# A routed feed-forward layer: constants built earlier, rows added per round of gathers, attention of four batches interleaved on three engines

## The reference

```python
x = x + 0.5 * _L0_ffn_ref(_layernorm(x), ...)   # first FFN
x = x + _L0_attn_ref(_layernorm(x), ...)        # full attention, 8 heads over 2048 tokens
x = x + 0.5 * _L0_ffn_ref(_layernorm(x), ...)   # second FFN

def _L0_ffn_ref(x, ...):                         # x: 8 batches, 2048 tokens, 256 wide
    scores = x @ w_router
    _, idx = jax.lax.top_k(scores, CAP)          # 128 tokens of each batch
    x_sel = jnp.take_along_axis(x, idx[:, :, None], axis=1)
    h = rmsnorm(x_sel, g1)
    q, k, v = ...                                # h @ W_qkv.T, 16 heads of 16
    att = softmax(where(mask, -inf, q @ k.T / 4))
    x_attn = (att @ v) @ W_out.T
    h2 = rmsnorm(x_sel + x_attn, g2)
    x_ff = silu(h2 @ W1.T) * (h2 @ W2.T) @ W3.T
    return x.at[..., idx].set(x_sel + x_attn + x_ff)
```

## Time and profile before

| | us |
|---|---|
| median of 3 runs | 4640.27 (4639.2 to 4641.36) |
| the profiled execution | 4629.35 |
| its span | 4627.6 |
| first `routed_ffn` in the span | 202.2 to 466.0 |
| second `routed_ffn` in the span | 4349.9 to 4627.6 |

### The profile page before, as it was taken

The page is one execution under the profiler, slowest core; times in us unless marked ns, Lnnn a source line. Parts: engine busy times, 40 slices in busy tenths (PEclk is TensorE's granted clock), DMA queues, the critical chain, the costliest instruction groups (busy, mean ns, idle before and its releaser), DMA issues. The chain is left out here.

```text
span 4627.6 us, 72033 instructions
## 1 busy us (share of the span) xinstructions
PE 3742.8 (81%) x21202; PEld 1462.9 (32%) x21202; DVE 3268.7 (71%) x4504; ACT 3216.1 (69%) x6587; POOL 2553.0 (55%) x966
## 2 busy tenths in 40 slices
PE   0176576599999999999999999999999999930276
PEld 0143354133333333333333333333333333310143
DVE  8644465777777877777777777778777777648544
ACT  5143365488888888878888887888888888834043
POOL 0011000377777777776777777677767777754111
PEclk9988788699999999999999999999999999965588
DMA  8200599677878878777887888788787877678100
GB/s 273 74 5 5 208 344 336 138 146 167 175 160 170 177 158 178 168 168 157 169 169 162 177 169 169 155 169 176 156 178 167 169 165 167 130 214 305 43 5 5
DMA packets 326047, 743.31 MB, mean 161 GB/s; under 512 B 26060, under 2 KB 209888, under 8 KB 270112
## 3 DMA queue, kind: packets, MB, share of 16 engines
q0 software_dynamic: 57216, 407.92, 44.3%
q1 hardware_dynamic: 234880, 297.04, 21.6%
q10 hardware_dynamic: 33568, 33.69, 2.1%
HBM read 198.90 MB, written 136.48 MB: 72 GB/s over the span
## 5 line engine op out<-in xcount | busy, mean ns | idle before, releaser
L1653 ACT ACTIVATE at_probs<-at_ps_s 128x512 f32<-128x512 f32 x4096 | 2255.7, 613 | 346.1 <-PE at_ps_s L1774 261.1
L1538 DVE TENSOR_REDUCE at_part_max<-at_ps_max 128x3 f32<-128x1536 f32 x1024 | 1801.0, 1759 | 472.3 <-PE at_ps_max L1687 464.2
L1516 POOL TENSOR_TENSOR at_pool_sum<-at_pool_sum,at_probs 128x2048 f32<-128x2048 f32 x384 | 1771.9, 4614 | 624.4 <-DMA at_probs<-at_probs 623.4
L1774 PE MATMUL at_ps_s<-at_qs,at_ks 97*128 97x512 f32 (+1 forms) x4096 | 1532.9, 452 | 41.2 <-ACT at_probs L1653 21.4
L1721 PE MATMUL at_ps_acc<-at_probs,at_v 128*32 128x512 f32 x8192 | 1097.5, 608 | 0.9 <-ACT at_probs L1653 0.9
L1774 PEld LDWEIGHTS at_ps_s<-at_qs,at_ks 97*128 97x128 f32 (+1 forms) x4096 | 629.8, 188 | 1151.2 <-ACT at_probs L1653 823.5
L1540 DVE TENSOR_REDUCE at_part_max<-at_max_copy 128x1 f32<-128x512 f32 x1024 | 691.6, 675 | 0.0
L1602 ACT COPY at_max_copy<-at_ps_max 128x512 f32<-128x512 f32 x1024 | 610.0, 596 | 88.1 <-PE at_ps_max L1687 87.6
L1687 PE MATMUL at_ps_max<-at_ks,at_qs 32*128 32x512 f32 x4096 | 525.9, 501 | 68.5 <-DMA at_ks<-qk_parts 34.8
L1493 POOL DMA_DIRECT2D at_probs<-at_probs x384 | 346.1, 901 | 220.6 <-PE at_ps_acc L1721 213.6
L1687 PEld LDWEIGHTS at_ps_max<-at_ks,at_qs 32*128 32x128 f32 x4096 | 198.1, 183 | 425.3 <-issue 363.9
(11 more groups left out here) (195 smaller groups left out, 2723.4 us busy)
## 6 DMA issues: line engine op xcount, KB each, us to landing
at_probs<-at_probs POOLq DMA_DIRECT2D x384, 1024.0 KB, 8.3
qk_parts<-pr_hi SPq DMA_DIRECT2D x32, 1024.0 KB, 6.4
qk_parts<-pr_lo SPq DMA_DIRECT2D x32, 1024.0 KB, 6.1
at_qs<-qk_parts SPq DMA_DIRECT2D x320, 64.0 KB, 6.0
at_ks<-qk_parts SPq DMA_DIRECT2D x80, 256.0 KB
s_x<-in_x SPq DMA_DIRECT2D x16, 1024.0 KB, 8.6
after_ffn<-s_y ACTq DMA_DIRECT2D x16, 1024.0 KB, 6.5
pr_x<-after_ffn SPq DMA_DIRECT2D x8, 2048.0 KB
```

The costliest lines, as they stand in the source:

```text
L1516: nc.gpsimd.tensor_tensor(acc, a, probs[:, c % RING], ALU.add).then_inc(pool_added, 1)
L1538: nc.vector.reduce_max(part_max[:, 0:HG - 1, t, c], ps_max[:, 0:HG - 1], AX.X).then_inc(three_max_done, 1)
L1653: nc.scalar.activation(probs[:, c % RING, h], ps_s[:, BANK[j]], ACT.Exp, scale=SCALE).then_inc(exp_done, 1)
L1774: nc.tensor.matmul(ps_s[:, BANK[j]], ks[rows, g, h, c * P:(c + 1) * P], qs[rows, un % NQB, h, :], start=True, stop=True).then_inc(scores, 1)
```

## The change

Three edits. The constants are tiles of `FfnWeights` and are built on GpSimd at the start of `pick_tokens`. In `routed_ffn` GpSimd gathers the four batches of round 0, adds them where there is something to add, and then does the same for round 1. In the attention part the order of the queues is changed: ScalarE takes the exponentials of slots 0, 1, 2, the copies of slot 0, the exponentials of slot 3, and the copies of slots 1, 2, 3; TensorE does the scores of slots 0, 1, 2, the probabilities of slot 0, the scores of slot 3, and the probabilities of slots 1, 2, 3; VectorE does `outputs(0)` and `outputs(1)` after `normalize(2)` and `normalize(3)`. VectorE also no longer waits for the weights at the start of `routed_ffn`.

```diff
+    def build(self, engine):
+        engine.memset(ones[:], 1.0).then_inc(self.built, 1)
+        engine.memset(zeros[:], 0.0).then_inc(self.built, 1)
...
@@ pick_tokens, gpsimd
             nc.gpsimd.tensor_copy(floats[:], ints[:]).then_inc(consts, 1)
+            weights.build(nc.gpsimd)
@@ routed_ffn, gpsimd
-            own = Chain(pool, consts)
-            own.step(nc.gpsimd.memset(ones[:], 1.0))
...
-            for i in range(ROUNDS):
-                for b in range(i * NB, i * NB + NB):
-                    if adding:
+                if adding:
+                    for b in range(i * NB, i * NB + NB):
                         pool.wait_ge(x_in[b], 32)
                         nc.gpsimd.tensor_tensor(xs[:, b, :], xs[:, b, :], ads[:, b, :], ALU.add
                                                 ).then_inc(rows_ready, 1)
@@ routed_ffn, vector
-            dve.wait_ge(consts, 6)
+            dve.wait_ge(weights.built, weights.BUILT)
...
-            dve.wait_ge(weights_in, WEIGHTS)
...
+                for s in range(NB):
+                    normalize(s)
+                    if s + 2 < NB:
+                        mask(s + 2)
+                    if s >= 2:
+                        outputs(s - 2)
+                for s in range(NB - 2, NB):
+                    outputs(s)
@@ routed_ffn, scalar
+                exponentials(0)
+                exponentials(1)
+                exponentials(2)
+                for s in range(NB):
+                    copy_turned(s)
+                    if s + 3 < NB:
+                        exponentials(s + 3)
@@ routed_ffn, tensor
+                for s in range(3):
+                    scores(s)
+                for s in range(NB):
+                    probabilities_v(s)
+                    if s + 3 < NB:
+                        scores(s + 3)
```

More of the change, by code:

```diff
@@ L294, in __init__ @@
                       sb("w2", [P, NC, DFF]), sb("w3", [P, DFF_TILES, D]), sb("gain", [P, 2, NC]))
+        GH = P // FD
+        self.consts = (sb("ident", [P, P]), sb("causal", [P, P]), sb("head_of", [P, GH]), sb("parity", [P, 2]))
+        self.scratch = (sb("ones", [P, P]), sb("zeros", [P, P]), sb("head_half", [P, GH]))
         used = ctx.enter_context(cleared_semaphores(nc))
         self.loaded = nc.alloc_semaphore(f"{tag}_loaded")
-        used.append(self.loaded)
+        self.built = nc.alloc_semaphore(f"{tag}_built")
+        used.extend((self.loaded, self.built))
+    BUILT = 6
+    def build(self, engine):
+        ident, causal, head_of, _ = self.consts
+        ones, zeros, head_half = self.scratch
+        GH = P // FD
+        engine.memset(ones[:], 1.0).then_inc(self.built, 1)
+        engine.memset(zeros[:], 0.0).then_inc(self.built, 1)
+        engine.wait_ge(self.built, 2)
+        engine.affine_select(out=ident[:], in_=ones[:], compare_op=ALU.is_equal, fill=0.0, base=0,
+                             pattern=[[-1, P]], channel_multiplier=1).then_inc(self.built, 1)
+        engine.affine_select(out=causal[:], in_=zeros[:], compare_op=ALU.is_ge, fill=-1e30, base=0,
+                             pattern=[[-1, P]], channel_multiplier=1).then_inc(self.built, 1)
+        engine.affine_select(out=head_half[:], in_=ones[:, 0:GH], compare_op=ALU.is_ge, fill=0.0, base=0,
+                             pattern=[[-FD, GH]], channel_multiplier=1).then_inc(self.built, 1)
+        engine.wait_ge(self.built, 5)
+        engine.affine_select(out=head_of[:], in_=head_half[:], compare_op=ALU.is_ge, fill=0.0, base=FD - 1,
+                             pattern=[[FD, GH]], channel_multiplier=-1).then_inc(self.built, 1)
     def load(self, queue):
@@ L488, in routed_ffn @@
         WEIGHTS = weights.COUNT
[L489 to L495, removed]
+        ident, causal, head_of, parity = weights.consts
         xs = sb("xs", [P, B, D])
@@ L519, in routed_ffn @@
         ps = ctx.enter_context(nc.psum_tensor(f"{tag}_ps", [P, 8, 512], F32))
-        consts = sem("consts")
         x_in = [sem(f"x_in{b}") for b in range(B)]
@@ L717, in _, with outputs @@
                 mask(1)
[L718 to L722, removed]
+                def outputs(s):
                     o = ps[:, BANK_O + s % 2, :].rearrange("p (g two t) -> p two g t", g=NC, two=2)
@@ L801, in _, with exponentials @@
                                ps[:, BANK_V:BANK_V + 2, :]).then_inc(v_copied, 1)
-                for s in range(NB):
+                def exponentials(s):
                     act.wait_ge(max_done, at(s))
@@ L807, in _, with copy_turned @@
                     last.then_inc(exp_done, 1)
-                for s in range(NB):
+                def copy_turned(s):
                     for half in range(2):
@@ L837, in _ @@
             pe.wait_ge(weights_in, WEIGHTS)
-            pe.wait_ge(consts, 6)
+            pe.wait_ge(weights.built, weights.BUILT)
             for i in range(ROUNDS):
@@ L866, in _, with scores @@
                 pe.wait_ge(v_copied, i + 1)
-                for s in range(NB):
+                def scores(s):
                     pe.wait_ge(spread_done, at(s))
@@ L876, in _, with probabilities_v @@
                     last.then_inc(scores_done, 1)
-                for s in range(NB):
+                def probabilities_v(s):
                     pe.wait_ge(dve_probs_done, at(s))
```

## The result

| | median us | runs | from–to |
|---|---|---|---|
| before, same chip | 4639.15 | 12 | 4634.95–4641.36 |
| after | 4652.4 | 12 | 4635.27–4662.08 |

The ratio after to before is 1.0026, with a 95% interval of 1.0015 to 1.0037: 13.3 us slower. Predicted were 4655.6 us (4645 to 4668), so 3.2 us more than came. The profiled execution took 4650.05 us (span 4648.3), 20.7 more than that of before, and this is what must be explained first. Windows by stage of the kernel after (columns as in the earlier trace rows): first FFN, full attention phase, second FFN.

The account below looks back on a forecast made before the run. GpSimd was taken to bound the second FFN's head, ScalarE, then its ping-pong with TensorE, attention from slot 2 on. Heads -18.7 and rounds +34.0 gave +15.3 us on 4640.3: 4655.6 us, range 4645 to 4668.

Parts of the forecast that it names:

- Heads: Start of both FFNs: early constants and gathers by round gain 5.8 us in the first, 12.9 in the second.
- Rounds: Attention rounds of both FFNs: `scores(3)` waits behind slot 0's probabilities, costing 8.5 us a round, +34.0 us over four.
- The first: Attention rounds: TensorE's clock also falls for `scores(3)`, 10.0 us a round, +21.3 us in all, 4661.6 us; chance 0.12.
- The second: FFN heads: VectorE's norm chain is held up beside gathers, 6.2 us less gain, +21.5 in all, 4661.8 us; chance 0.08.
- The third: Attention rounds: interleaving works, `scores(3)` and `mask(3)` come early, 2 us less a round, -26.7 in all, 4613.6 us; chance 0.05.
- The fourth: Heads' gain and rounds' loss nearly cancel, loss under 7 us a round, +5 us in all, 4645.6 us; chance 0.08.

Follow-up runs that it names:

- heads alone: The changed kernel with the attention queue order of before; early constants and rows added per round of gathers stay: 4619.27 us against 4638.24, ratio 0.9961.
- constants alone: The changed kernel with the old attention queue order and all gathers ahead of all additions; constants still built early: 4631.5 us, ratio 0.9984.
- outputs late: The changed kernel with VectorE's four `outputs` put back behind all `normalize`: 4645.21 us, ratio 1.0015.
- order alone: The kernel before with only the new order of the three attention queues: 4669.78 us, ratio 1.0075.
- scores first: The changed kernel with slot 3's scores put back ahead of slot 0's probabilities on TensorE: 4609.94 us, ratio 0.9952.
- two threaded kernels: The changed kernel, slot 0's turnings around `scores(3)`, its copies between exponentials: 4603.78 us; then also slot 3's exponentials halved, a slot 1 copy behind each: 4589.82 us.

## Why the prediction was right, and which term was not

**Heads, -18.7.** Right. To the end of the norm it was -5.8 and -12.8 us in the trace, and the kernel with the heads alone gained 19.0 (with 3.2 us of TensorE's clock in its profile, as told below). Behind the norm 0.9 us was given back in the first FFN: 16 matmuls of K and Q took 10.20 us in place of 9.35, so the spread of K came 5.0 us earlier and not 5.8. These 16 took anything from 9.0 to 10.2 us in the seven kernels with this head, so the 0.9 us is no fixed price of it.

**Rounds, +34.0.** The mechanism was right in every step, and the experiments show it: taking back TensorE's queue alone removes the stall. The size was 2.5 us short. From the third mask to the first matmul of the gated layer the rounds took 9.1, 8.8, 9.4 and 9.3 us longer, 36.5 in all. Of the 2.5 us, 1.4 arise up to the last `outputs` and 1.1 between it and the gated layer.

**The mis-sized term: what the clock does to the rest, taken as nothing.** I wrote that up to slot 2's exponentials nothing moves, and that projection and gated layer follow as before. The sum of the two FFNs of both profiles closes only with these:

| piece, both FFNs | predicted us | in the trace us |
|---|---|---|
| to the spread of K | -18.7 | -17.7 |
| third mask to gated layer, four rounds | +34.0 | +36.5 |
| first to third mask, first rounds | 0 | -3.1 |
| first to third mask, second rounds | 0 | -3.4 |
| gated layer and what follows | 0 | -3.5 |
| sum | +15.3 | +8.8 (windows: +8.8) |

The last three are the same instructions at another clock: shorter by 10 us. For that reason the FFNs took 270.9 and 279.6 us, where the prediction named about 275 and 282.

The -3.1 belongs to this one execution more than to the change. It stands in the first round of the first FFN, and there it comes and goes between kernels whose first FFN is the same: heads alone (masks 6.15 us apart) has it, constants alone (7.84) hasn't, nor has the change with the outputs late (7.8). Without it the trace says +11.9, and the medians say +13.3.

The -3.4 goes with the order. In the second rounds slot 2's scores took 3.67 us in all eight profiled rounds of the change, the order alone, scores first and outputs late, and 5.34 to 5.37 in all six of the old order (before, heads alone, constants alone), though TensorE's own queue up to there is the same. The two threaded kernels, which take slot 0's copies earlier still, took 5.17 to 5.37, so copies ahead of slot 3's exponentials alone don't bring it. The -3.5 goes the same way: the 24 matmuls of the gated layer took 12.07 to 12.62 us in the 16 rounds of the first group, 12.71 to 13.15 in the threaded ones and 13.06 to 13.45 in the old order. What in the round before sets this, no experiment tells: the cause stays open.

**How near, and how much of it is luck.** The mechanism and its sign were foreseen, and the experiments bear them out. That the median came within 2.0 us of the forecast change (+13.3 for +15.3) is in part luck: the heads gave 1.0 us less and the rounds cost 2.5 more than reckoned, and the clock terms taken as nothing gave back 6.9 (the -3.4 and the -3.5) to 10 us.

**Rivals.** The first (clock down for `scores(3)`) is out: 3.70 us in all four rounds. The second is out: beside gathers the `tensor_scalar` took 0.17 us, one of them 0.23, and the gathers stayed at 0.94 to 0.96 with 0.30 us between. The Trainium skill (SBUF — State Buffer, "Who interferes with whom") lets a `tensor_scalar` in a two-port mode and GpSimd exclude each other; at 128x4 nothing of it is seen beyond that 0.06 us, and whether these ran in such a mode no run shows. Its other rule, two SBUF inputs beside a GpSimd that reads, agrees with the 0.65 us of the constants alone. The third has the mechanism that sets in once `scores(3)` moves up. Its -26.7 us is near the -28.3 measured there by luck: its rounds gave 3.1 us and not 8, and TensorE's clock the rest. The fourth named a loss of under 7 us a round; it was 9.1.

## What to carry to other kernels

An engine's queue is in order, so interleaving pays only if the start of the slowest cross-engine chain (here scores, mask, maxima, exponentials: 8.6 us before ScalarE can begin) is ahead of everything that waits for the engine that it feeds. Put the producer early in its queue, then fill the consumer's queue with short pieces of the ping-pong between its long ones: half a slot's exponentials (3.1 us) hide a turning even when it takes 1.97 us. When a reordering changes where TensorE idles, look at the duration of each burst behind it before calling those parts unmoved.

## Unexpected of the hardware

The same eight matmuls took 3.67 or 5.37 us, and 24 in a row 12.30 or 13.31, as the granted clock stood; over both FFNs this gave back 10 us that no changed instruction explains. The 16 matmuls of K and Q in the first FFN took 10.20 us after and 9.35 before while the granted clock reads 1.00 in both windows, and in the second FFN of the kernel before they took 9.42 us at a reading of 0.75, so that column doesn't tell all of TensorE's pace. And a phase of 3300 us with the same instructions varied by 15 us between single executions, more than most effects studied here.
